# Delta heads: the second merge level as pairs of 32x32 products, with the products and weight turns around it in another order

## The reference, cut to what matters

```python
q, k, v = silu(causal_conv4(x @ Wq.T)), silu(causal_conv4(x @ Wk.T)), silu(causal_conv4(x @ Wv.T))
q, k = q / |q|, k / |k|
g, beta = exp(-exp(A_log) * softplus(a + dt_bias)), sigmoid(b)
# for each token t, S is 128x128 and starts at zero
error = v_t - g_t * (S.T @ k_t)
S = g_t * S + outer(k_t, beta_t * error)
o_t = S.T @ q_t
# then: o = o * rsqrt(mean(o*o)) * norm_w * silu(x @ Wg.T); result o @ Wo.T
```

## Time and profile before

| | |
|---|---|
| median of three runs | 3422.26 us (3414.85 to 3426.41) |
| the profiled execution, its own time | 3415.16 us |
| its span in the profile | 3413.4 us |
| mean granted TensorE clock over the span | 0.981 |
| delta heads in steady state | 130 to 1715 us of the span |
| TensorE / VectorE / ScalarE / GpSimd busy, whole span | 3180.1 / 2191.9 / 1898.9 / 1672.6 us |

### The profile page before, as it was taken

One profiled execution on the slowest core, in us unless ns is written; L12 is line 12 of the kernel. 1 busy time (PEld: TensorE's weight loads), 2 busy tenths in 40 slices (PEclk: granted clock), 3 DMA queues, 4 the chain that ended last, 5 costly groups with the idle time before them and its releaser, 6 DMA issues. The chain is left out here.

```text
span 3413.4 us, 60026 instructions
## 1 busy us (share of the span) xinstructions
PE 3180.1 (93%) x18834; PEld 2544.9 (75%) x18834; DVE 2191.9 (64%) x4849; ACT 1898.9 (56%) x4657; POOL 1672.6 (49%) x3107
## 2 busy tenths in 40 slices
PE   6899999999999999999999788799979999998998
PEld 3688888888888888888878555488866777776543
DVE  5577777777777777777653488765547567574432
ACT  3677777777777777777532377644445445363111
POOL 2777787777788777778630000145534002011322
PEclk9899999999999999999999999999989999999999
DMA  4222222222222222222353333423351222211854
GB/s 113 63 73 69 59 69 62 73 68 67 74 55 73 62 73 68 65 76 53 97 176 92 115 142 142 177 87 103 115 174 57 68 69 69 93 65 53 271 99 56
DMA packets 432408, 310.47 MB, mean 91 GB/s; under 512 B 130496, under 2 KB 347456, under 8 KB 431072
## 3 DMA queue, kind: packets, MB, share of 16 engines
q1 hardware_dynamic: 423792, 289.57, 28.8%
q0 software_dynamic: 8432, 18.88, 2.8%
HBM read 177.97 MB, written 130.43 MB: 90 GB/s over the span
## 5 line engine op out<-in xcount | busy, mean ns | idle before, releaser
L631 PE MATMUL gd_PJ<-xn_lead,gd_w_rest 128*128 128x512 f32 x1024 | 421.3, 411 | 0.5 <-DVE gd_w_rest L786 0.5
L631 PE MATMUL gd_PJ<-xn_lead,gd_w_lead 128*128 128x512 f32 x1024 | 403.0, 394 | 0.0
L631 PE MATMUL gd_PJ<-xn_rest,gd_w_lead 128*128 128x512 f32 x1024 | 401.9, 393 | 0.0
L1079 POOL TENSOR_TENSOR gd_prod<-gd_L,gd_T 32x14 f32<-32x14 f32 (+6 forms) x896 | 324.8, 362 | 70.4
L1082 POOL TENSOR_TENSOR gd_T<-gd_T,gd_prod 32x14 f32<-32x14 f32 (+6 forms) x896 | 311.6, 348 | 71.6 <-POOL gd_prod L1079 2.5
L793 DVE SCALAR_TENSOR_TENSOR gd_conv<-gd_pre,gd_cur_a,gd_conv 128x512 f32<-128x512 f32 x384 | 301.8, 786 | 13.3 <-ACT gd_conv L958 2.9
L631 PEld LDWEIGHTS gd_PJ<-xn_lead,gd_w_lead 128*128 128x128 f32 x1024 | 193.8, 189 | 43.4
L631 PEld LDWEIGHTS gd_PJ<-xn_lead,gd_w_rest 128*128 128x128 f32 x1024 | 194.4, 190 | 38.5 <-DVE gd_w_rest L786 0.9
L631 PEld LDWEIGHTS gd_PJ<-xn_rest,gd_w_lead 128*128 128x128 f32 x1024 | 194.6, 190 | 35.3
L932 DVE SCALAR_TENSOR_TENSOR gd_og<-gd_B,ptab,gd_gate 128x512 f32<-128x512 f32 x64 | 48.1, 751 | 243.8 <-PE gd_B L645 243.8
L2619 ACT ACTIVATE sa_E<-sa_B,sa_nmax 128x512 f32<-128x512 f32 (+3 forms) x256 | 131.3, 525 | 131.4 <-DVE sa_nmax L2756 127.2
(11 more groups left out here) (476 smaller groups left out, 8620.3 us busy)
## 6 DMA issues: line engine op xcount, KB each, us to landing
expert_rows<-xt_blank SPq DMA_DIRECT2D x16, 2112.0 KB, 7.3
turned_queries_keys<-f_wq SPq DMA_DIRECT2D x16, 1280.0 KB, 6.0
x_wo<-decay_sums SPq DMA_DIRECT2D x64, 256.0 KB, 3.7
triangles<-gd_Lo SPq DMA_DIRECT2D x64, 256.0 KB, 3.5
gd_W<-turned_image SPq DMA_DIRECT2D x64, 256.0 KB
gd_T<-inverse_image SPq DMA_DIRECT2D x64, 256.0 KB
gated_outputs<-gd_og SPq DMA_DIRECT2D x64, 256.0 KB, 2.8
go_ogt<-gated_outputs SPq DMA_DIRECT2D x16, 1024.0 KB, 5.9
```

The lines of the kernel that those rows point to most:

```text
L631: mm = pe.matmul(bank, w_parts[wp][:, j, k, :], rhs, start=(k == 0 and wp == 1), stop=(k == KT - 1 and wp + xp == 0))
L1079: nc.gpsimd.tensor_tensor(prod[:, rows, 0:j], L16[:, rows, j:j + 1].to_broadcast(shape), T16[:, j:j + 1, 0:j].to_broadcast(shape), ALU.mul ...
```

## The change

1. Level 1 (32 to 64). Instead of full products, each sequence has two products of 32x32, one for each pair of blocks of 32: at rows 0 to 63 and at rows 64 to 127. The first pair's results go to bank 2 (or 3), the second pair's to bank 0, which is otherwise used for the transposes of o. Signs and copies are done for the two quarters separately, `turned_blocks` and `turned_corner` write a new tile `inv` (zeroed once) instead of `T`, and only the parts that are read. TensorE adds one to a semaphore `blocks_open` between the waits and the first small product.
2. Order on TensorE. For c > 0, q S and merge 1 now stand ahead of keys by keys; before, keys by keys and merge 1 stood ahead of q S. For c = 0, spread 2 stands between the two halves of the v projection.
3. Weight turns. Wk, Wq and Wg are turned behind the v projection, in slots 1, 2 and 3, all into bank 1 of `PJ`; Wv stays where it was, in slot 2. Before, Wk was turned in slot 1 ahead of spread 1, Wq in slot 3 ahead of spread 0 and Wg in slot 3 ahead of the v projection.
4. Order on VectorE and ScalarE. `turned_blocks` and R stand ahead of the last key tap; `merged(1)` and `turned_corner` directly behind `masked(1)`; the diagonal and its sum behind all q taps; `merged(2)` ahead of the key norms; the rests of weights behind the scaled keys. On ScalarE the square root stands behind q's silu, and the leads behind that.

```diff
@@ buffers and names
+        inv = sb("inv", [P, B, TOP + TOP // 2])
+        SIDE = MERGE[1]
+        PAIRS = ((0, half[2]), (2 * SIDE, Bk[0][:, :, 0:SIDE]))
+        UPPERS = ((0, half[3]), (2 * SIDE, Bk[0][:, :, SIDE:2 * SIDE]))
+        TURN_BANK = (1, 0, 1, 1)
+        W_TURN = (1, 3, 2, 4)
@@ TensorE, spread_rows
+                    elif l == 1:
+                        pe.wait_ge(og_ready, n + 1)
+                        pe.sem_inc(blocks_open, 1)
+                        for b in range(B):
+                            for q, bank in PAIRS:
+                                lo, hi = slice(q, q + SIDE), slice(q + SIDE, q + 2 * SIDE)
+                                mm = pe.matmul(bank[lo, b, 0:SIDE], Lo_c[hi, b, lo], W_c[hi, b, hi], start=True, stop=True)
+                        mm.then_inc(y_sum, 1)
@@ TensorE, merge
+                    pe.wait_ge(inv_ready, n * (NM - 1) + l)
+                    if l == 1:
+                        pe.sem_inc(blocks_open, 1)
+                        for b in range(B):
+                            for q, bank in UPPERS:
+                                at = slice(q, q + SIDE)
+                                mm = pe.matmul(bank[at, b, 0:SIDE], inv[at, b, q:q + SIDE], Y[at, l % 2, b, 0:SIDE], start=True, stop=True)
+                        mm.then_inc(wup, 1)
                     else:
-                        each(half[3][0:TOP], [T_c[:, b, 0:TOP] for b in range(B)], [Y[:, l % 2, b, :] for b in range(B)], wup)
-
-                if back and more and c == CH - 1:
-                    pe.wait_ge(g_silu, n + 2)
-                    turn_weights(h1, JQ)
+                        each(half[3][0:TOP], [inv[:, b, 0:TOP] for b in range(B)], [Y[:, l % 2, b, :] for b in range(B)], wup)
@@ TensorE, slot
-                if back and more and c == 1:
-                    pe.wait_ge(k_pre, n + 3)
-                    turn_weights(i + 1, JK)
                 if back:
                     spread_rows(1)
+                    if c > 0:
+                        pe.wait_ge(r_ready, i * (CH - 1) + c)
+                        each(Bk[1], q_c, tiles(S), oi_sum)
+                        merge(1)
                 if has2:
                     pe.wait_ge(k_silu, n + 3)
                     if has1:
                         pe.wait_ge(lo_ready, n + 2)
                     each(Bk[4], k_c, k_c, kk_done)
-                if back:
+                if back and c == 0:
                     merge(1)
-                    if c > 0:
-                        pe.wait_ge(r_ready, i * (CH - 1) + c)
-                        each(Bk[1], q_c, tiles(S), oi_sum)
+                if back and c > 0:
                     spread_rows(2)
-                if back and more and c == CH - 1:
-                    pe.wait_ge(q_pre, n + 2)
-                    turn_weights(h1, JG)
...
+                    pe.wait_ge(w_copied, h1 * 4 + W_TURN[JV] if back else 4)
+                    if back and c == 0:
+                        project(JV, c1, v_proj, range(0, KT // 2))
+                        spread_rows(2)
+                        project(JV, c1, v_proj, range(KT // 2, KT))
                     else:
-                        pe.wait_ge(w_copied, h1 * 4 + JV + 1)
-                    project(JV, c1, v_proj)
+                        project(JV, c1, v_proj)
+                if back and more and c > 0:
+                    pe.wait_ge(q_pre, n + 2)
+                    turn_weights(i + 1, (JK, JQ, JG)[c - 1])
                 if back:
                     merge(2)
@@ VectorE, masked and merged
+                    if l == 1:
+                        for q, bank in PAIRS:
+                            at = slice(q, q + SIDE)
+                            ts = nc.vector.tensor_scalar(Y[at, l % 2, :, 0:SIDE], bank[at, :, 0:SIDE], -1.0, None, ALU.mult)
+                        ts.then_inc(y_ready, 1)
+                        return
...
+                    if l == 1:
+                        for q, bank in UPPERS:
+                            tc = nc.vector.tensor_copy(W_c[q:q + SIDE, :, q + SIDE:q + 2 * SIDE], bank[q:q + SIDE, :, 0:SIDE])
+                        tc.then_inc(w_ready, 1)
+                        return
...
-                    nc.vector.transpose(T_c, W_c).then_inc(t_next, 1)
+                    nc.vector.transpose(inv[0:TOP, :, 0:TOP], W_c[0:TOP, :, 0:TOP])
+                    at = slice(2 * SIDE, 3 * SIDE)
+                    nc.vector.transpose(inv[at, :, at], W_c[at, :, at]).then_inc(inv_ready, 1)
...
-                    nc.vector.transpose(T_c[s:2 * s, :, 0:s], W_c[0:s, :, s:2 * s]).then_inc(t_next, 1)
+                    nc.vector.transpose(inv[SIDE:2 * SIDE, :, 0:SIDE], half[3][0:SIDE, :, 0:SIDE]).then_inc(inv_ready, 1)
@@ VectorE, slot
                 if back:
                     merged(0)
-                if has2:
-                    tap(n + 2, par, PK, cur_k, (2,), k_tap)
+                    turned_blocks()
...
+                if has2:
+                    tap(n + 2, par, PK, cur_k, (2,), k_tap)
                 if back:
-                    turned_blocks()
                     masked(1)
+                    merged(1)
+                    turned_corner()
                 if has1:
                     dve.wait_ge(q_halo, n + 2)
                     dve.wait_ge(q_pre, n + 2)
                     tap(n + 1, parm, PQ, cur_a, (0,), q_tap)
-                if back and more and c == 1:
-                    rest_weights(i + 1, JK)
+                if back:
+                    masked(2)
+                if has1:
+                    tap(n + 1, parm, PQ, cur_a, (1, 2), q_tap)
                 if has2:
                     dve.wait_ge(kk_done, n + 3)
...
                 if back:
-                    turned_corner()
-                    masked(2)
-                if has1:
-                    tap(n + 1, parm, PQ, cur_a, (1, 2), q_tap)
+                    merged(2)
                 if has2:
                     dve.wait_ge(k_root, n + 3)
...
-                if back:
-                    merged(2)
-                if has2:
                     dve.wait_ge(scales_done, n + 3)
...
-                if back and more and c == CH - 1:
-                    rest_weights(h1, JG)
+                if back and more and c > 0:
+                    rest_weights(i + 1, (JK, JQ, JG)[c - 1])
@@ ScalarE, slot
-                if back and more and c == 1:
-                    lead_weights(i + 1, JK)
-                if has2:
-                    act.wait_ge(k_len, n + 3)
-                    nc.scalar.activation(klen[:, :], kss[:, :], ACT.Sqrt).then_inc(k_root, 1)
...
                     silu(PQ, qT[:, parm, :], q_silu)
-                if back and more and c == CH - 1:
-                    lead_weights(h1, JG)
+                if has2:
+                    act.wait_ge(k_len, n + 3)
+                    nc.scalar.activation(klen[:, :], kss[:, :], ACT.Sqrt).then_inc(k_root, 1)
+                if back and more and c > 0:
+                    lead_weights(i + 1, (JK, JQ, JG)[c - 1])
```

80 lines of the change are left out of this document (36 added, 44 removed).

## The result

| | before | after |
|---|---|---|
| median of 7 runs each, on the same chip | 3418.89 us (3414.85 to 3428.81) | 3435.28 us (3426.08 to 3439.01) |
| ratio | | 1.004, 95% interval 1.0025 to 1.0054 |
| the profiled execution, its own time | 3415.16 us | 3432.86 us |
| its span | 3413.4 us | 3431.0 us |

The account below looks back on a forecast made before the run. It took a once-per-head loop through PE, DVE, POOL and a DMA as the bound. Terms 0.81 + 0.35 + 0.20 - 0.12 = +1.24 us a head, x 15 = +18.6 us, gave 3440 us, range 3402 to 3474.

Parts of the forecast that it names:

- the loop for the kernel before: Once per head: PE slots 1 to 3, DVE's L903 in slot 3, POOL through slot 0, DMA, next slot 1.
- I take 40 ns: the fp32 line, somewhat lower: Level-1 products on PE: 40 ns per small record, a group 0.82 us against 0.84, -0.12 us a head.
- rival 1: Level-1 products: two array corners run side by side, 13 ns a record, -20 us in all, 3402 us; chance 0.24.
- my own formula: Change per head from p ns per small record: -2.61 + 0.096 p us; p = 40 gives +18 us in all.
- the sum has 20: Order's delays per head: norms +0.81, slot 2 +0.35, q S order +0.20 us, over 15 heads.
- the 0.35 and the 0.2: Delays per head: +0.35 us in slot 2 from later weight rests, +0.2 us for q S between the groups.
- the DMA wait: PE's wait for the solved blocks ahead of slot 1, once per head: would grow from 0.7 to 1.5 us or more.
- the two reasons that I named: If slot 1's DMA wait shrinks: POOL's slot 0 start doesn't follow L903, or POOL got faster because DVE disturbs it less.
- +0.35 us in slot 2, between 0 and 0.6: Slot 2: weight rests delay L903, POOL, the next head's parameters, ACT and DVE, so PE waits +0.35 us a head.
- I booked nothing, with the DMA wait as cover: Slot 0: v projection's second half covers a copy PE waited 0.52 us for; gain goes into the DMA wait: 0.
- DVE's smaller pieces: 0: On DVE, the transpose and masked multiplies split into pairs take about as long in sum: 0.
- The +0.81 us of the norms: DVE, slot 3: four small key-norm operations moved behind the third merge's copy delay L903, +0.81 us a head.

Follow-up runs that it names:

- e5: Kernel before plus two extra, unused VectorE reductions in slot 3 ahead of the query norms (L903): 3439.84 us, ratio 1.006.
- e2: Kernel after with the full level-1 products and their old functions, so the new order alone: 3449.33 us, ratio 1.0096.
- e3: Kernel after with VectorE's last key tap moved ahead of the small transposes, in slot 0 only: 3423.53 us, ratio 1.0026.
- e8: e1 with VectorE's second merge ahead of the key diagonal and, in slot 0, the last level's first product behind the first v-projection half: 3422.93 us, ratio 1.0005.
- e12: e8 with ScalarE's q S copy ahead of the square root, slot 2's transposes and masked(1) ahead of R, idle products in the last slot: 3413.38 us, ratio 0.9995.
- e7: Kernel after plus four idle identity products on TensorE ahead of slot 0's key product: 3428.92 us, ratio 1.0034.
- e1: Kernel before with only the small 32x32 products and their split copies, old order kept: 3428.84 us, ratio 1.0044.
- e11: Kernel after plus 22 idle identity products where TensorE waits in the last head's last slot: 3428.39 us, ratio 1.0023.
- e4: Kernel after with VectorE's first merge and small transposes ahead of the first key tap, in slot 2 only: 3435.75 us, ratio 1.0059.

## Why the prediction was right and wrong

**Right.** The direction, the size (+16 us between the medians, +17.7 between the profiled executions, for +18), and that less work on PE would not be less time. Right too was the loop for the kernel before (e5). Slots 1 and 3 gained about what the products and the vanished wait give; slots 2 and 0 lost more. The size itself was luck: two terms were wrong by some 12 to 17 us each, in opposite directions.

**Wrong: the price of a small record.** "I take 40 ns: the fp32 line, somewhat lower" was the failed choice. A group of 16 is 0.44 us with 0.194 for one (groups view), so (0.44 - 0.194) / 15 = 16 ns apart, near the 13 of rival 1. That fits its mechanism, two corners of the array side by side, but no run had the small products in one corner only, so it is not shown that the corners are the reason. By my own formula -2.61 + 0.096 x 16 = -1.1 us a head, 16 us *faster*. So the two errors cancelled: the products gained some 0.4 us a group where I had 0.02 (14 to 19 us in all for 2), and the order cost 33 us (e2) where the sum has 20. (In rival 1, "under 30 if the 0.35 and the 0.2 don't come" is a slip: by the formula 10 us faster needs p under 26 then.)

**Wrong in kind: the DMA wait.** I had written that it would grow to 1.5 us or more and that I am wrong in kind if it goes. It went, in all 14 heads. (That it stood in 15 was a misreading of the earlier trace rows: the longest, 4.16 us, was PE's first wait of all.) Of the two reasons that I named for such a case the second holds, but neither is the main one. The last DMA of the blocks was issued 2.15 us before the end of slot 0 and is now issued 4.63 before it (means of 14 heads). Some 2.1 us of that difference are that PE's slot 0 has become longer; 0.4 that the issue comes earlier in the slot. That fits e3, where slot 0 is 0.75 us longer than before and one head waits, and e8 and e12, where slot 0 is as short as before (23.13 and 23.15) and the wait stands in all 14.

**Wrong in size: slot 2.** "+0.35 us in slot 2, between 0 and 0.6". The chain was read right, L929 late, POOL late, `cur_k` late, ACT, DVE, but not whom it meets: PE arrives sooner and needs R *before* the key product. PE waits 0.7 us there in twelve heads and 1.2 to 1.4 in three, and slot 2 is 0.91 longer.

**Missed: slot 0.** I booked nothing, with the DMA wait as cover. The two transposes now ahead of the last key tap make silu of k late; PE, which has nothing else to do, waits 1.1 to 1.7 us in 14 heads, and in five of 15 slots the clock falls behind that. e3 takes most of the first away, and the falls with it (12 us between the medians), e7 the second (6 us).

**Missed: "DVE's smaller pieces: 0".** +0.33 us a slot (e1).

**Missed: the tail.** +6.4 us in the last slot, mostly the clock behind a wait; e11 gives 5 of it back.

**The +0.81 us of the norms** came as forecast, and was undone behind it. From PE's third merge product of slot 3 to L903 were 4.91 us (819.10 to 824.01 in the head shown), in the kernel after they are 5.73 in the same head and in the mean:

```profile
819.10 0.68 PE L640 MATMUL gd_B<-gd_Y,gd_T 128*64 128x64 f32 x8
```

```profile
921.31 0.68 PE L647 MATMUL gd_B<-gd_Y,gd_inv 128*64 128x64 f32 x8
...
927.04 0.16 DVE L929 TENSOR_SCALAR gd_qss<-gd_qss 128x4 f32<-128x4 f32 x1
```

From the start of slot 3 L929 starts 19.14 us in for 19.30, since PE's part ahead of it has become shorter by 1.0. What I had taken as fixed is the other half of the loop: from L903 to the last DMA issue were 27.17 us and are 25.97. POOL's 28 steps of a solve (L1079 and L1082, now L1102 and L1105) take 9.14 us in slot 0, where they took 10.96. In the kernel before, one of these steps outside and one inside a stretch of DVE's convolution taps:

```profile
835.78 0.24 POOL L1082 TENSOR_TENSOR gd_T<-gd_T,gd_prod 32x26 f32<-32x26 f32 x1
...
844.58 2.31 DVE L793 SCALAR_TENSOR_TENSOR gd_conv<-gd_pre,gd_cur_a,gd_conv 128x512 f32<-128x512 f32 x3
...
846.26 0.72 POOL L1082 TENSOR_TENSOR gd_T<-gd_T,gd_prod 32x26 f32<-32x26 f32 x1
```

Of the steps that begin while DVE does a tap, 308 of 352 take over 0.15 us more than the shortest of their shape; of all others, 57 of 1440. In the kernel after it is 284 of 298 and 61 of 1494. Slot 0 had 7 such long steps among its 28, now 4: the new order moved the taps against the solve. So POOL's pace goes with where DVE's taps stand; that is read from the traces, no run moved the taps alone. The prediction named it only as a way of being wrong.

**Open.** Why a head stays at 99.2 to 99.7 us under so different orders. POOL is busy for 1172 of the 1489 us of e12's heads and waits another 114 us for the triangle's round trip and for the length of q. That speaks for the chain through POOL. In the kernels in which PE waits for the DMA in every head (before, e5, e8, e12) the distance from L903 of slot 3 to the first product of slot 1 is the same to 0.3 us (30.4 to 30.7); what sets the rest of the head, and the heads of the other kernels, is argued and not shown: no run here made POOL's own work shorter over a whole head.

## What to carry to other kernels

Where PE waits for DVE, ACT or a DMA once per slot, a cheaper group of products is worth only what the next chain allows. Read for each slot which release would come next, in distances from a fixed point and over several slots, and not from the length of the present wait: in e4 one release was exchanged for another that came at the same time, and in e5 a chain that was 1.2 us later made its wait only 0.35 us longer. A list of waits over a window can hold a first or a last wait that belongs to no loop; look each case up in the timeline. An operation on a helper engine is worth moving by what stands behind it: one swap of a tap and a transpose was worth some 12 us by the slots. And on PE a wait costs more than its length when the clock falls behind it, so fill unavoidable ones with work.

## What was not expected of the hardware

- Products of 32x32 in fp32, two corners of the array in turn: 16 ns in the mean from record to record, where full ones of 64 columns stood 105 ns apart and those with 64 weight columns 65 ns.
- The granted clock fell to the 1.2 GHz level behind a wait of 1.44 us and came back some 3 us later. Four idle products (1.16 us together) in that gap kept it up in all 15 slots 0 of e7, and 22 in the last slot saved 5 us there (e11).
- On VectorE a scale or copy of 32x128 took 0.28 us, one of 128x256 with a mask 0.42 us: the two quarters cost more than the whole.
- The same step of POOL's solve took 0.24 us, and 0.72 when it began while DVE did a convolution tap (a SCALAR_TENSOR_TENSOR of 128x512).
